# First attention: the guess of the roots in five VectorE steps, and the output bias as a one-row product

## The reference, cut to what matters

```python
xn = layernorm(x)                                  # over 256, eps 1e-5
q = ln16(xn @ Wq + bq)                             # 16 heads of 16: layernorm per head, eps 1e-6, then * w + b
k = ln16(ctx_main @ Wk + bk); v = ctx_main @ Wv + bv          # 48 keys of a sequence
k_dca, v_dca = ln16(...), ...  of ctx_dca @ Wkv_dca + bkv_dca  # the last 16 keys
o = softmax(q k^T / 4) v + softmax(q k_dca^T / 4) v_dca       # two softmaxes, summed
x = x + o @ Wo + bo
x = x + ffn0(layernorm(x)); x = x + xattn1(layernorm(x), ctx_1024); x = x + ffn1(layernorm(x))
```

## Time and profile before

| what | value |
|---|---|
| median of 3 runs | 749.72 us (747.78 to 749.95) |
| the profiled execution | 747.85 us, span 746.0 us, mean granted clock 0.979 |
| PE busy over the span | 668.1 us (90%) |
| DVE busy | 556.2 us (75%) |
| ACT busy | 480.1 us (64%) |
| POOL busy | 442.4 us (59%) |
| L409, 16 instructions | 13.3 us, 830 ns mean |
| L411, 16 instructions | 7.3 us, 453 ns mean |
| L413, 16 instructions | 2.9 us, 184 ns mean |
| L620, 16 instructions | 11.7 us, 729 ns mean |

### The profile page before, as it was taken

How to read it: one execution, slowest core, us unless ns; L and a number is a source line. 1 busy time by engine, 2 the same in 40 slices (tenths; PEclk the granted TensorE clock), 3 DMA queues, 4 the chain that set the end, 5 groups by cost and what they waited for, 6 DMA issues and landing times. The chain is left out here.

```text
span 746.0 us, 16279 instructions
## 1 busy us (share of the span) xinstructions
PE 668.1 (90%) x5782; PEld 532.3 (71%) x5782; DVE 556.2 (75%) x1212; ACT 480.1 (64%) x982; POOL 442.4 (59%) x648
## 2 busy tenths in 40 slices
PE   2778888877999989999999999999999999978794
PEld 1556666655888877888888888888888888765452
DVE  3699999996578886768677777676777666746886
ACT  1467767664556667666666666666666666657994
POOL 2487787876677744656666666666656564535500
PEclk9999999996999999999999999999999999999996
DMA  8200000400410000000010000000000000000001
GB/s 285 61 9 9 9 8 12 169 1 2 127 58 29 8 15 1 16 22 16 15 29 9 22 23 22 23 16 15 29 9 15 15 2 1 1 1 1 29 29 58
DMA packets 26019, 22.83 MB, mean 31 GB/s; under 512 B 5041, under 2 KB 24402, under 8 KB 25810
## 3 DMA queue, kind: packets, MB, share of 16 engines
q1 hardware_dynamic: 24160, 20.92, 8.9%
q10 hardware_dynamic: 1778, 0.86, 0.4%
HBM read 19.67 MB, written 2.10 MB: 29 GB/s over the span
## 5 line engine op out<-in xcount | busy, mean ns | idle before, releaser
L683 POOL TENSOR_TENSOR rstd<-var,minus_half 128x8 f32<-128x8 f32 x65 | 107.7, 1657 | 5.1
L674 POOL TENSOR_TENSOR p_n<-pr,pinv 128x256 f32<-128x256 f32 x64 | 39.3, 613 | 79.6 <-DVE pinv L915 79.6
L659 POOL TENSOR_TENSOR pr<-pr,rstd 128x256 f32<-128x256 f32 x64 | 39.2, 613 | 78.7 <-DVE pr L954 78.7
L1565 PE MATMUL banks<-m_hi,z_hi 128*128 128x256 f32 x256 | 74.4, 291 | 7.5 <-DVE z_lo L907 7.5
L1193 ACT ACTIVATE kT<-banks,gk_q 128x512 f32<-128x512 f32 x64 | 44.0, 688 | 50.6 <-PE banks L1574 50.6
L1565 PE MATMUL banks<-m_hi,z_lo 128*128 128x256 f32 x256 | 72.1, 282 | 0.0
L1565 PE MATMUL banks<-m_lo,z_hi 128*128 128x256 f32 x256 | 72.0, 281 | 0.0
L907 DVE TENSOR_TENSOR z_lo<-banks,z_hi 128x512 fp32r<-128x512 f32 x64 | 43.9, 686 | 31.2 <-ACT z_hi L1159 31.2
L934 DVE TENSOR_REDUCE sums<-q_sq 128x4 f32<-128x512 f32 x64 | 43.7, 683 | 25.8 <-ACT q_sq L1174 25.7
L950 DVE TENSOR_REDUCE pmax<-banks 128x4 f32<-128x256 f32 x64 | 27.0, 422 | 46.3 <-PE banks L1610 46.3
L1565 PEld LDWEIGHTS banks<-m_hi,z_hi 128*128 128x128 f32 x256 | 48.3, 189 | 17.3 <-DVE z_lo L907 15.9
(11 more groups left out here) (189 smaller groups left out, 2087.8 us busy)
## 6 DMA issues: line engine op xcount, KB each, us to landing
w_raw<-in_L_xattn_Wq SPq DMA_DIRECT2D x4, 512.0 KB, 5.5
wo_raw<-in_L_xattn_Wo SPq DMA_DIRECT2D x1, 2048.0 KB, 8.3
k_ctx<-in_ctx SPq DMA_DIRECT2D x16, 128.0 KB, 2.7
w_raw<-in_L_ffn_w_gating SPq DMA_DIRECT2D x16, 128.0 KB, 2.4
out_x<-x_sb SPq DMA_DIRECT2D x4, 512.0 KB, 3.0
x_sb<-in_x SPq DMA_DIRECT2D x1, 1536.0 KB, 9.2
a_ctx<-in_ctx SPq DMA_DIRECT2D x16, 64.0 KB, 1.7
w_raw<-in_L_xattn_Wk SPq DMA_DIRECT2D x2, 512.0 KB, 8.9
```

Source lines behind the costliest of these rows:

```text
L674: pool.tensor_tensor(p_n[:, 1 - par, :, :], pr[:, 1 - par, :, :], pinv[:, 1 - par, :].unsqueeze(2).to_broadcast([P, HC, S]), ALU.mult).the ...
L683: pool.tensor_tensor(rstd1[:, par, :], var1[:, :], minus_half[:, :].to_broadcast([P, 2 * HC]), ALU.pow).then_inc(root1, 1)
L1565: last = nc.tensor.matmul(bank[6][:, za * D:(za + 1) * D], z[:, odd, c, :], mm[:, h, :], start=w % NS == 0 and c == 0 and m == 0, stop=w % ...
```

## The change

The squares are made by ACT with a factor inside (SQ_SCALE = sqrt(0.5/16)), and written into rows of 17 places whose last holds 0.5 * eps, set once by POOL. The sum over 17 places is then half of the mean square plus half of eps, and is written straight to half2. The guess takes the bits of half2 times -0.5 plus the constant in one instruction, so that L409 and L411 fall away. The bias leaves POOL: PE begins each y with a product of a row of ones (1x128) and the bias row (1x256), and the four old matmuls add to it. PE now waits for x_updated ahead of this product, and for o_evac behind it. Three POOL memsets are added before the loop: a row of ones, the column of 0.5 * eps, and v_blk2 (128x512), which nothing reads; ACT waits for four counts of zeros where it waited for three. The places of the other tensors in SBUF stay as they were.

```diff
-        LN_N, NEWT_N = 7, 8
+        LN_N, NEWT_N = 5, 8
...
-            dve.tensor_scalar(half, total, 0.5 / HD0, 0.5 * QK_EPS, ALU.mult, ALU.add).then_inc(ln_steps, 1)
+            dve.tensor_scalar(y.bitcast(U32), half.bitcast(U32), -0.5, RSQRT_MAGIC_HALF, ALU.mult, ALU.add).then_inc(ln_steps, 1)
             dve.wait_ge(ln_steps, base + 1)
-            dve.tensor_scalar(y.bitcast(U32), half.bitcast(U32), 1, None, ALU.logical_shift_right).then_inc(ln_steps, 1)
+            dve.tensor_tensor(tmp, y, y, ALU.mult).then_inc(ln_steps, 1)
             dve.wait_ge(ln_steps, base + 2)
-            dve.tensor_scalar(y.bitcast(U32), y.bitcast(U32), -1.0, RSQRT_MAGIC_HALF, ALU.mult, ALU.add).then_inc(ln_steps, 1)
+            dve.scalar_tensor_tensor(tmp, tmp, -1.0, half, ALU.mult, ALU.mult).then_inc(ln_steps, 1)
             dve.wait_ge(ln_steps, base + 3)
-            dve.tensor_tensor(tmp, y, y, ALU.mult).then_inc(ln_steps, 1)
-            dve.wait_ge(ln_steps, base + 4)
-            dve.scalar_tensor_tensor(tmp, tmp, -1.0, half, ALU.mult, ALU.mult).then_inc(ln_steps, 1)
-            dve.wait_ge(ln_steps, base + 5)
             dve.scalar_tensor_tensor(y, tmp, 1.5, y, ALU.add, ALU.mult).then_inc(ln_steps, 1)
...
+            pool.memset(ones_row[0:1, :], 1.0).then_inc(ones_set, 1)
+            pool.memset(v_blk2[:], 0.0).then_inc(zeros, 1)
+            pool.memset(qk_sq[:, :, HD0:HD0 + 1], 0.5 * QK_EPS).then_inc(eps_set, 1)
...
-                t = i - 1
-                if live(t, NT):
-
-                    if t == 0:
-                        pool.wait_ge(bo_ready, 1)
-                    pool.wait_ge(xhat_ready, t + 1)
-                    pool.tensor_tensor(x_sb[:, t, :], x_sb[:, t, :], bo_bc[:, :], ALU.add).then_inc(x_biased, 1)
...
+                    if t == 0:
+                        dve.wait_ge(eps_set, 1)
                     dve.wait_ge(sq_ready, t + 1)
                     after(dve, scaled, t - 1)
-                    dve.tensor_reduce(qk_mean[:, :], qk_sq[:, :, :], AX.X, ALU.add).then_inc(ln_steps, 1)
+                    dve.tensor_reduce(half2[:, t % 2, :, 0], qk_sq[:, :, :], AX.X, ALU.add).then_inc(ln_steps, 1)
...
                     dve.wait_ge(y_done, t + 1)
-                    dve.wait_ge(x_biased, t + 1)
...
-            act.wait_ge(zeros, 3)
+            act.wait_ge(zeros, 4)
...
-                    act.activation(qk_sq[:, :, :], qk_cent[:, t % 2, :, :], ACT.Square).then_inc(sq_ready, 1)
+                    act.activation(qk_sq[:, :, 0:HD0], qk_cent[:, t % 2, :, :], ACT.Square, scale=SQ_SCALE).then_inc(sq_ready, 1)
...
+                    if t == 0:
+                        pe.wait_ge(bo_ready, 1)
+                        pe.wait_ge(ones_set, 1)
+                    after(pe, x_updated, t)
+                    nc.tensor.matmul(y_bank(t)[:, 0:D], ones_row[0:1, :], bo_bc[0:1, :], start=True, stop=False)
                     pe.wait_ge(o_evac, t + 1)
-                    after(pe, x_updated, t)
                     for kk in range(KD):
-                        last = nc.tensor.matmul(y_bank(t)[:, 0:D], oT[:, kk, :], wo0[:, kk, :], start=kk == 0, stop=kk == KD - 1)
+                        last = nc.tensor.matmul(y_bank(t)[:, 0:D], oT[:, kk, :], wo0[:, kk, :], start=False, stop=kk == KD - 1)
```

More of the change, by code:

```diff
@@ L40 @@
 SCALE0 = HD0 ** -0.5
+SQ_SCALE = (0.5 / HD0) ** 0.5
 PAD = 32
@@ L206, in build @@
         rnd2 = sb(sa, "rnd2", [P, 2, W_CHUNK, 2])
-        r_room = sb(sa, "r_room", [P, 6 * D])
+        v_blk2 = sb(sa, "v_blk2", [P, PER, H // 2, 2 * HD0])
+        qk_sq = sb(sa, "qk_sq", [P, 2 * H, HD0 + 1])
+        r_room = sb(sa, "r_room", [P, 480])
         bo_bc = sb(sa, "bo_bc", [P, D])
@@ L222, in build @@
         prm = sb(sa, "prm", [P, D])
-        b_room = sb(sa, "b_room", [P, 128])
+        ones_row = sb(sa, "ones_row", [P, P])
         a_cT = sb(sa, "a_cT", [P, 2, 2, PER, S])
         qk_cent = sb(sa, "qk_cent", [P, 2, 2 * H, HD0])
-        qk_sq = sb(sa, "qk_sq", [P, 2 * H, HD0])
+        s_room = sb(sa, "s_room", [P, 2 * D])
         qk_norm = sb(sa, "qk_norm", [P, 2 * H, HD0])
@@ L302, in build @@
         wo_in, prm_in, bo_in, cols_done, cols_ready = sem("wo_in"), sem("prm_in"), sem("bo_in"), sem("cols_done"), sem("cols_ready")
-        bv_ready, bo_done, bo_ready, row_negated, warm = sem("bv_ready"), sem("bo_done"), sem("bo_ready"), sem("row_negated"), sem("warm")
+        bv_ready, bo_done, bo_ready, row_negated, warm, eps_set = sem("bv_ready"), sem("bo_done"), sem("bo_ready"), sem("row_negated"), sem("warm"), sem("eps_set")
         consts = sem("consts")
@@ L320, in build @@
         o_done, o_evac, y_done = sem("o_done"), sem("o_evac"), sem("y_done")
-        x_biased, x_updated = sem("x_biased"), sem("x_updated")
+        ones_set, x_updated = sem("ones_set"), sem("x_updated")
         stored = sem("stored")
@@ L405, in newton_steps, with first_guess @@
                 pool.tensor_tensor(y, y, tmp, ALU.mult).then_inc(newton, 1)
-        def first_guess(dve, base, half, total, y, tmp):
-            dve.tensor_scalar(half, total, 0.5 / HD0, 0.5 * QK_EPS, ALU.mult, ALU.add).then_inc(ln_steps, 1)
+        def first_guess(dve, base, half, y, tmp):
+            dve.tensor_scalar(y.bitcast(U32), half.bitcast(U32), -0.5, RSQRT_MAGIC_HALF, ALU.mult, ALU.add).then_inc(ln_steps, 1)
             dve.wait_ge(ln_steps, base + 1)
-            dve.tensor_scalar(y.bitcast(U32), half.bitcast(U32), 1, None, ALU.logical_shift_right).then_inc(ln_steps, 1)
+            dve.tensor_tensor(tmp, y, y, ALU.mult).then_inc(ln_steps, 1)
             dve.wait_ge(ln_steps, base + 2)
-            dve.tensor_scalar(y.bitcast(U32), y.bitcast(U32), -1.0, RSQRT_MAGIC_HALF, ALU.mult, ALU.add).then_inc(ln_steps, 1)
+            dve.scalar_tensor_tensor(tmp, tmp, -1.0, half, ALU.mult, ALU.mult).then_inc(ln_steps, 1)
             dve.wait_ge(ln_steps, base + 3)
-            dve.tensor_tensor(tmp, y, y, ALU.mult).then_inc(ln_steps, 1)
-            dve.wait_ge(ln_steps, base + 4)
-            dve.scalar_tensor_tensor(tmp, tmp, -1.0, half, ALU.mult, ALU.mult).then_inc(ln_steps, 1)
-            dve.wait_ge(ln_steps, base + 5)
             dve.scalar_tensor_tensor(y, tmp, 1.5, y, ALU.add, ALU.mult).then_inc(ln_steps, 1)
@@ L752, in step @@
                 if live(t, NT):
+                    if t == 0:
+                        dve.wait_ge(eps_set, 1)
                     dve.wait_ge(sq_ready, t + 1)
                     after(dve, scaled, t - 1)
-                    dve.tensor_reduce(qk_mean[:, :], qk_sq[:, :, :], AX.X, ALU.add).then_inc(ln_steps, 1)
+                    dve.tensor_reduce(half2[:, t % 2, :, 0], qk_sq[:, :, :], AX.X, ALU.add).then_inc(ln_steps, 1)
                     dve.wait_ge(ln_steps, LN_N * t + 1)
-                    first_guess(dve, LN_N * t + 1, half2[:, t % 2, :, 0], qk_mean[:, :], rstd2[:, t % 2, :, 0], qk_tmp[:, t % 2, :])
+                    first_guess(dve, LN_N * t + 1, half2[:, t % 2, :, 0], rstd2[:, t % 2, :, 0], qk_tmp[:, t % 2, :])
                 for c in chunks(i):
```

## The result

The changed kernel takes **745.99 us** (median of 12 runs, 744.69 to 748.38) against 750.11 for the kernel before beside it (12 runs, 747.78 to 751.64). The ratio is 0.9954, interval 0.9941 to 0.9967: 3.4 us less by the ratio, 2.5 to 4.4 (4.1 by the two medians). Forecast were 741.4 us and 8.3 us less. So the sign was right and the gain forecast was more than twice the one measured; the time lies just inside the upper edge of the range, 746.

The account below looks back on a forecast made before the run. DVE was taken to bound the tile step. Savings of 5.4 (guess) + 1.7 (ramp) + 0.5 (L430) - 0.2 (last product) = 7.4 us gave 740.4 or 742.3 by base; forecast 741.4 us, range 737 to 746.

Parts of the forecast that it names:

- DVE bounds the step: Steady tile steps: DVE shows no wait and sets the 9.33 us step, which falls to 8.88 us with DVE still the bound.
- Two steps off the guess are worth 0.45 us per tile: Guess on DVE, steady tiles: only two steps' spacing is saved, 0.44 to 0.45 us each, 5.4 us over twelve tiles.
- The held product: Product of y by itself on DVE: held until POOL's second division part ends, about S + 2.17, rather than running free in 0.19.
- rival 1: Guess on DVE: the product of y runs free beside POOL, saving 0.80 us per tile, total 737.2 us; chance 0.15.
- L430 free of L620 at the end: End of the stage: L430 no longer stands behind POOL's bias addition and takes 0.29 instead of 0.80, 0.51 us gained.
- Bias on PE: Sixteen one-row products on PE, 0.22 us each: free in steady steps, costing 0.22 us, up to 0.45, at the last y.
- The cover of 0.68 us: PE's idle time per steady step, waiting for the keys, hides the bias product; without it the cost is 3.5 us.
- Rival 4: Bias product on PE costs 0.38 us and delays y in all sixteen tiles, 6.1 us more, total 747.5 us; chance 0.06.
- Ramp 1.7 us: First tiles of the stage: shorter guess and earlier division start gain 1.7 us, with 0.8 and 2.5 as ends.
- The base: Starting time for the subtraction: profiled execution 747.85 us gives 740.4, median 749.72 gives 742.3; forecast set between them.
- Rival 3: PE's clock rises later after the shifted stage end: 10 us later costs 5 us, 20 us gives 751.5 us; chance 0.04.

Follow-up runs that it names:

- bias_only: The kernel before with its seven-step guess kept and the output bias as a one-row product on PE: 751.84 us, ratio to the kernel before 1.0009.
- double_product: The changed kernel with the one-row bias product issued twice for each tile: 748.55 us, ratio to the kernel before 0.9981.
- the fastest one: The changed kernel with guess in PSUM, fp32r bias product and last y not waiting for x_updated: 738.08 us; with unread transposes added, 735.33 us.

## Why the prediction was right, and where it failed

- *DVE bounds the step*: right. 8.89 us per step (8.88 foreseen), DVE without waits in the stretch.
- *Two steps off the guess are worth 0.45 us per tile, not the 1.5 us that the profile shows on them*: right, to 0.01 us. The held product was the fork, and it went as L878 said; rival 1, the free product, fell (0.55, not 0.19). The Trainium skill's rule for two SBUF inputs ("SBUF — State Buffer", "Who interferes with whom") agrees with the product of y: 0.55 us beside the division with both inputs in SBUF, 0.19 with one of them in PSUM. It does not fit POOL's power, which holds no such step (below).
- *L430 free of L620 at the end*: right in mechanism, where the clock is up. L429 takes 0.30 there after the change, 0.80 before, and tile 15's maxima come 9.75 us after tile 14's instead of 10.19; in the second profile, with the clock low, 11.22.

```profile
167.33 0.30 DVE L429 TENSOR_SCALAR rnd<-w_raw 128x256 uint32<-128x256 uint32 x1 [2.01 <-POOL w L615]
```

- *Bias on PE, 0.22 us each, hidden but for the last*: **this step failed.** I took each of the four records in 1.03 us for a product; but a y of two fp32 products shows as x4, so one product is two records and 0.63 us, 1.15 at the lower clock (bias_only, 168.21 to 169.36). The cover of 0.68 us was right for the steady step, and that is why the steps are as foreseen. But with 0.63 of 0.68 used, nothing was left where PE runs at 1.2 GHz, as the step to the last maxima shows. Foreseen for all products 0.2 us, measured 1.3 to 1.9, and none that can be measured with the transposes in. With the 0.5 us for L430 and up to 0.6 in the ramp the sum had the move of the bias as a gain of 0.3 to 0.9 us; it is a loss. Rival 4 named the mechanism, with a price (6.1 us) for failing everywhere. Open is how the price divides between the last steps and episodes like the one at 146 us.
- *Ramp 1.7 us*: too large, and a cost beside it was left out. With the held guess of tile 3 the sum had 2.1 us up to that tile's maxima; at the same clock the profiles show 1.4, so about 1.0 for the ramp, within the 0.8 to 2.5 given. In both profiles of the changed kernel the low clock took it back.
- *The base*: the profiled execution (747.85) was a short one; eleven to twenty-three runs of the kernel before have medians of 750.1 to 751.1. The forecast between 740.4 and 742.3 should have gone by the median. That is another 1 us.
- *Rival 3, slower by the clock*: the sign was wrong, but the clock took part of the gain, at the ramp by about 1.9 us, and in the last steps.
- Several misses in one direction brought the total to the edge of the range; that it still lies inside, by 0.01 us, is luck.

## What to carry to other kernels

When an instruction looks long, ask what it waits for before counting what its removal gives: L409 and L411 showed 1.5 us and were worth 0.45, and only moving an operand to PSUM got at the rest. Count records per operation before dividing a group's time, fp32 products above all. A cover must be checked at both clock levels, and at the ends of a stage as well as in its middle; what just fits at 2.4 GHz can be late at 1.2. And profiles of two kernels are compared at the same granted clock, or the clock is read as the change.

## What the runs showed of the hardware that was not expected

- A product with one input row is no cheaper than one with 128. In fp32, over 256 columns at 2.4 GHz, two one-row products in double_product start 0.53 us apart (108.05 and 108.58), and y starts 0.63 us after the product in the changed kernel; the two 128-row products of a y take 1.03 to 1.13 us together. In fp32r the one-row product takes 0.31.
- POOL's power of -1/2 on 128x4 doesn't hold DVE, though it lasts 1.03 us: in the kernel before L415, L419 and L430 run at their shortest, 0.19 and 0.29 us, while it goes. POOL's timeline there:

```profile
106.33 1.03 POOL L449 TENSOR_TENSOR row_rstd<-row_v,minus_half 128x4 f32<-128x4 f32 x1
```

- Transposes that nobody reads, put into PE's waits, raised the granted clock of the ramp (25 to 40 us) from 0.66 to 0.89 in the profiles without them to 1.00 in all three with them. By the medians they brought 2.3 us in the changed kernel (745.80, the mean of its two medians, to 743.47) and 2.8 in the fastest one (738.08 to 735.33), but nothing in the kernel with the guess alone; the intervals of each pair of ratios overlap, so the size of this gain stays open.
